# Low-part value matmuls gathered behind a tile's last bank, in an eight-head attention with layer norm in split fp32

## The reference

```python
# x (2048, 256), adj (2048, 2048), Wq, Wk, Wv (256, 2048), Wout (2048, 256), all float32
q = (x @ Wq).reshape(8, 2048, 256)      # likewise k and v
a = einsum('hnd,hmd->hnm', q, k) / 16 + adj + adj
mask = adj == 0
a = softmax(where(mask, -1e6, a)); a = where(mask, 0, a)
out = einsum('hnm,hmd->hnd', a, v).transpose(1, 0, 2).reshape(2048, 2048)
result = layernorm(x + out @ Wout)      # over the last axis, eps 1e-5
```

## Time and profile before

| | |
|---|---|
| median of 3 runs | 1827.27 us (1826.62 to 1828.08) |
| the profiled execution's own time | 1826.6 us, the lowest of the three; its span is the same 1826.6 us |
| busy, share of the span | PE 98%, weight loads 87%, DVE 61%, POOL 54%, ACT 47% |
| PE idle before a value matmul, waiting for POOL's low part | 8.1 us in 7 places |

### The profile page before, as it was taken

One profiled execution on the slowest core, in us unless ns is written; L12 is line 12 of the kernel. 1 busy time (PEld: TensorE's weight loads), 2 busy tenths in 40 slices (PEclk: granted clock), 3 DMA queues, 4 the chain that ended last, 5 costly groups with the idle time before them and its releaser, 6 DMA issues.

```text
span 1826.6 us, 29365 instructions
## 1 busy us (share of the span) xinstructions
PE 1798.8 (98%) x10272; PEld 1582.2 (87%) x10272; DVE 1122.2 (61%) x2318; ACT 852.8 (47%) x1411; POOL 984.9 (54%) x762
## 2 busy tenths in 40 slices
PE   8998989999999999999999999999999999999998
PEld 7887789888898889988899888988889888898887
DVE  6888855665555565555555666555555566546667
ACT  5654554444454445444454444544444444544433
POOL 7878864544644555444554555644455454554443
PEclk9999999999999999999999999999999999999999
DMA  7788875666656666466664666657665566655664
GB/s 250 249 251 267 257 211 154 192 191 195 178 157 185 191 195 186 142 198 194 189 188 142 199 188 190 183 153 201 190 180 173 162 198 196 187 159 169 171 178 140
DMA packets 186995, 345.97 MB, mean 189 GB/s; under 512 B 39392, under 2 KB 96736, under 8 KB 170464
## 3 DMA queue, kind: packets, MB, share of 16 engines
q10 hardware_dynamic: 92032, 200.59, 35.5%
q1 hardware_dynamic: 94816, 143.50, 28.5%
HBM read 190.84 MB, written 18.87 MB: 115 GB/s over the span
## 4 chain that ended last, share of the span: by engine, by line
PE 85%; DVE 1%; SPq 0%; issue 0%; ACT 0%; ACTq 0%; DMA 0%; DVEq 0%
PE bank L400 34%; PE y_bank L417 22%; PE bank L365 17%; PE y_bank L420 12%; SPq L304 0%; DVE y_acc L742 0%; DVE blocks L654 0%; ACTq L567 0%; PE bank L385 0%; DVE p_split L748 0%; DVE y_acc L677 0%; DMA p_turned<-blocks 0%; DVE y_acc L674 0%; ACT m_sb L558 0%; DVE ln L714 0%
## 5 line engine op out<-in xcount | busy, mean ns | idle before, releaser
L471 POOL TENSOR_TENSOR p_split<-p_turned,p_split 128x512 fp32r<-128x512 f32 x510 | 649.7, 1303 | 579.2 <-ACT p_split L539 578.9
L400 PE MATMUL bank<-k_split,q_split 128*128 128x512 f32 x3072 | 794.7, 394 | 0.0
L400 PEld LDWEIGHTS bank<-k_split,q_split 128*128 128x128 f32 x3072 | 546.2, 190 | 90.2
L417 PE MATMUL y_bank<-v_split,p_split 128*128 128x512 f32 x2048 | 549.1, 390 | 8.6 <-POOL p_split L471 8.1
L631 DVE CUSTOM_DVE_ANT_0 t_p<-bank,m_sb 128x512 f32<-128x512 f32 x512 | 350.8, 687 | 231.7 <-PE bank L400 204.5
L417 PEld LDWEIGHTS y_bank<-v_split,p_split 128*128 128x128 f32 x2048 | 382.6, 188 | 92.4 <-POOL p_split L471 11.0
L530 ACT ACTIVATE t_p<-t_p,small 128x2048 f32<-128x2048 f32 x128 | 257.0, 2008 | 392.7 <-DVE small L643 392.7
L460 POOL TENSOR_TENSOR w_slot<-raw_w,w_slot 128x512 fp32r<-128x512 f32 x192 | 250.5, 1305 | 220.7 <-ACT w_slot L510 217.4
L654 DVE STREAM_TRANSPOSE blocks<-t_p 128x2048 f32<-128x2048 f32 x128 | 295.9, 2311 | 97.6 <-ACT t_p L530 77.9
L420 PEld LDWEIGHTS y_bank<-v_split,p_split 128*128 128x128 f32 x2048 | 313.5, 189 | 40.2
L539 ACT ACTIVATE p_split<-p_turned 128x512 fp32r<-128x512 f32 x512 | 287.7, 620 | 86.9 <-DMA p_turned<-blocks 82.8
(11 more groups left out here) (44 smaller groups left out, 644.4 us busy)
## 6 DMA issues: line engine op xcount, KB each, us to landing
m_sb<-m_dram ACTq DMA_DIRECT2D x112, 1024.0 KB, 5.2
p_turned<-blocks SPq DMA_DIRECT2D x1532, 64.0 KB, 2.2
p_turned<-blocks ACTq DMA_DIRECT2D x516, 64.0 KB, 2.8
blocks<-in_adj_dram SPq DMA_DIRECT2D x64, 256.0 KB, 4.2
raw_w<-in_L_gnn_Wv_dram ACTq DMA_DIRECT2D x64, 256.0 KB, 3.4
m_dram<-m_sb SPq DMA_DIRECT2D x16, 1024.0 KB, 6.4
raw_w<-in_L_gnn_Wq_dram ACTq DMA_DIRECT2D x63, 256.0 KB, 3.3
raw_w<-in_L_gnn_Wk_dram ACTq DMA_DIRECT2D x61, 256.0 KB, 4.0
```

The source lines that it names most:

```text
L400: mm = nc.tensor.matmul(dst[:], q[:, a, k, f * P:(f + 1) * P], k_split[:, kk, k, b * BANK:(b + 1) * BANK], start=(i == 0), stop=(i == len( ...
L417: nc.tensor.matmul(y[:], p_split[tau % 2][:, HI, j * P:(j + 1) * P], v_split[:, j].rearrange("p s d -> p (s d)"), start=(j == 0), stop=False)
L471: nc.gpsimd.tensor_tensor(lo, p_turned[:, i * BANK:(i + 1) * BANK].rearrange("p (j b) -> p j b", b=QUAD), hi.bitcast(F32), ALU.subtract).t ...
```

## The change

Three things move; no arithmetic is added or left out, and every matmul keeps its operands.

1. `values` is cut in two. `values_hi` does the wide matmuls in each slot as before and, in slot 0, waits for P's four high parts (`p_hi`) where the four low parts were waited for. `values_lo` does the narrow ones: all 16 of a tile behind the wide ones of slot 3, with the wait for the low parts in front. Only the last tile of a head (but for the very last) keeps four narrow ones in each slot, because v is overwritten there.
2. A head's q projections stand in slot 3 of the even tiles in place of slot 1, and the next head's first q in slot 3 of tile 14 in place of slot 2. They come behind the 16 narrow value matmuls.
3. In later heads the first vt moves from slot 2 of tile 1 to slot 3, in front of the second.

Since `due` orders every engine's work, ACT, DVE and POOL handle the moved projections at the new places too, and the banks of the ring and the weight slots are dealt out in the new order.

```diff
+LO_EVERY = 4
...
-        LATER_V = {(1, 2): (("vt", 0),), (1, 3): (("vt", 1),), (2, 0): (("v", 0), ("vt", 2), ("v", 1), ("vt", 3)),
+        LATER_V = {(1, 3): (("vt", 0), ("vt", 1)), (2, 0): (("v", 0), ("vt", 2), ("v", 1), ("vt", 3)),
...
-            if t % 2 == 0 and t <= LAST_Q and b == (2 if tau == 0 else 1):
+            if t % 2 == 0 and t <= LAST_Q and b == (2 if tau == 0 else 3):
                 yield "q", h, t // 2 + 1
...
-                if (t, b) == (TILES - 2, 2):
+                if (t, b) == (TILES - 2, 3):
                     yield "q", h + 1, 0
...
-                def values(tau, g):
+                def values_hi(tau, g):
                     h, t = divmod(tau, TILES)
                     y = y_bank[tau % 2]
                     if g == 0:
-                        pe.wait_ge(p_lo, 4 * (tau + 1))
+                        pe.wait_ge(p_hi, 4 * (tau + 1))
...
+                def values_lo(tau, first, last):
+                    y = y_bank[tau % 2]
+                    if first == 0:
+                        pe.wait_ge(p_lo, 4 * (tau + 1))
+                    for j in range(TPB * first, TPB * (last + 1)):
                         mm = nc.tensor.matmul(y[:, 0:D], p_split[tau % 2][:, LO, j * P:(j + 1) * P],
                                               v_split[:, j, HI], start=False, stop=(j == CHUNKS - 1))
-                    if g == BANKS - 1:
+                    if last == BANKS - 1:
                         mm.then_inc(y_done, 1)
+
+                def values(tau, g):
+                    values_hi(tau, g)
+                    if tau % TILES == TILES - 1 and tau < ALL - 1:
+                        values_lo(tau, g, g)
+                    elif g % LO_EVERY == LO_EVERY - 1:
+                        values_lo(tau, g + 1 - LO_EVERY, g)
```

More of the change, by code:

```diff
@@ L414, in values @@
                         wait_emptied(("v", h, 2 * g + 1))
-                    chunks = range(TPB * g, TPB * (g + 1))
-                    for j in chunks:
+                    for j in range(TPB * g, TPB * (g + 1)):
                         nc.tensor.matmul(y[:], p_split[tau % 2][:, HI, j * P:(j + 1) * P],
                                          v_split[:, j].rearrange("p s d -> p (s d)"), start=(j == 0), stop=False)
-                    for j in chunks:
+                def values_lo(tau, first, last):
[3 more added lines that the diff above has]
+                    for j in range(TPB * first, TPB * (last + 1)):
                         mm = nc.tensor.matmul(y[:, 0:D], p_split[tau % 2][:, LO, j * P:(j + 1) * P],
                                               v_split[:, j, HI], start=False, stop=(j == CHUNKS - 1))
-                    if g == BANKS - 1:
+                    if last == BANKS - 1:
                         mm.then_inc(y_done, 1)
+                def values(tau, g):
[4 more added lines that the diff above has]
+                        values_lo(tau, g + 1 - LO_EVERY, g)
                 pe.wait_ge(ident_ready, 1)
```

## The result

| | before | after |
|---|---|---|
| median, us | 1827.04 (21 executions, 1824.4 to 1829.27) | 1830.92 (21 executions, 1827.68 to 1836.71) |
| span of the profiled execution, us | 1826.6 | 1827.1 |

The ratio is 1.0022, with a 95% interval of 1.0016 to 1.0028: slower by 3.9 us, where 1.7 was forecast. It is inside the range, at the edge between "within 0.2%" and "slower".

A forecast was written before the change was run, and what follows sets the result against it. PE, busy 98% of the span, was taken as the bound. 1826.6 - 5.4 + 3.6 + 3.0 + 0.5 = 1828.3 us, and 1828.9 for the median; range 1823.5 to 1834.0.

The forecast's parts named there:

- Fewer changes of width: From k2 on, 270 narrow runs among wide matmuls go, each saving about 0.02 us: 5.4 us gained, between 4.5 and 6.
- The rival that nothing is saved: Wide matmuls take as long whatever went before, so grouping gives nothing: 1834.3 us, chance 0.12.
- The wait before k2 at the later ends: Moved q delays ACT's exponential and k2's weight: 0.6 us at six ends of heads 2 to 7, 3.6 us; bounds 0 to 7.2.
- The moved q in the first head: Copies on ACT and DVE delay transposes in tiles 4 and 10 and tile 14's exponential: k2 3.0 us late, bounds 0 to 5.6.
- the forecast's +3.5: First-head loss: 3.0 us by which k2 is late, plus 0.5 us for a longer stretch of low clock.
- the "over 8": Sign of being right: PE idle over 8 us before k2 in the first head.
- The clock: Low-clock stretch at the first head's end may last longer: 0.5 us added, between 0 and 1.7.
- The wait for the high parts: Seven first-head waits end earlier, 3.6 us at one place, but PE then waits for k2's weight: costed at nothing.
- one sign of being wrong: Waits of PE for DVE, a bank or q not emptied, in even tiles.
- What costs nothing: Later heads' other q's (exponential about 1.3 us later, P wanted two tiles on), the moved vt and the tail: no cost.
- the rival "more waits than counted": Weights behind k2's late too (+3.6 us) and first head at its bound (+2.6): up to 1835 us, chance 0.15.

The follow-up runs named there:

- the change with both edits: The full change plus weights split one key earlier and DVE's denominator at slot 2 instead of 0: 1819.95 us, 0.9957 against the kernel before.
- the order alone: Kernel before with only the projections moved (q's, next head's first q, first vt), values as before: 1831.9 us, ratio 1.0027.
- the values alone: Kernel before with values grouped and waiting for high parts, projections unmoved: 1828.19 us, 1.0002; with weights one key earlier 1825.19; with denominator at slot 2 too 1821.07.
- before with the same two edits: Kernel before with weights split one key earlier and DVE's denominator at slot 2 instead of 0: 1822.44 us, ratio 0.9981.
- the whole change: The full change with weights split one key earlier: 1825.99 us, 0.999 against the kernel before; with the denominator at slot 2 too, 1819.95, 0.9957.

## Why the prediction was right and wrong

**Fewer changes of width: right, in mechanism and size.** 0.78 us a head was forecast (39 x 0.02), and the change with both edits shows 222.82 against 223.59. Six scores behind wide value matmuls take 1.36 us, behind narrow ones 1.39. The rival that nothing is saved is refuted. The Trainium skill's page "TensorE: Matmul & The Clock Gate", section "Back-to-back issue gap", gives the formula that the prediction quoted for an isolated matmul, with nothing for what went before; the trace differs from it by the 0.03 us on entry. With the projections at their old places the saving is 0.62 (222.97): seven of the eight q's, and the first vt, stand between wide matmuls there, and each makes a change of width of its own, 8 x 0.02 = 0.16.

**The wait before k2 at the later ends: right.** 0.6 us forecast, 0.56 at every undisturbed end, with the exponential at 1.2 and POOL's weight ahead, as worked out. 223.46 a head is the free 222.82 plus this wait and a little for its weight load.

**The moved q in the first head: right at each place, not in the sum.** From the row maximum to the transpose, the order alone took 4.70, 4.54, 4.85 and 3.48 us in tiles 4, 8, 10 and 14, where before took 3.12, 3.26, 3.42 and 2.52; in tiles 6 and 12, which waited for DMAs, nothing was added. But the 3.0 us on k2 did not show: 233.83 in one execution, in which SP began the shuffles of tile 8 at 152.46, right behind the transpose, where before had held them for 1.5 us; 236.43 in another. k2 was 0.5 us earlier than in before, and 1.8 and 2.1 later. The start of the second head, -1.0, +4.0 and +4.3 us against before in three executions, has the forecast's +3.5 inside its spread, but partly by luck: in the two late ones half of it is the clock's. So this term stands for a mean at best; the profiled execution of after, taken alone, would have called it wrong. PE's idle time before k0 to k2 was 7.6, 7.0 and 5.6 us, less than the "over 8" that was to be the sign.

**The clock: too small in two of three.** 0.5 us was added, 1.7 at most. The low stretch at the first head's end was 3.4 us long in before and in the first profile of after, but 10.2 in the other two, and from k2 to the second head's start they took 16.5 us, where before took 14.3: 2.2 us.

**The wait for the high parts "at nothing": probably too low.** The medians put it at some 3 to 4 us, a gain, with the reserve said above. I argued that none of what paces the first head waits for PE, so that k2's weight alone decides where PE gets to; and I left out that a wait in mid-head can put the next microseconds at half rate. If the gain is real, the total came out near because the next point took it back, which is luck. And one sign of being wrong did show: PE now waits for DVE in four slots of the first head, where before had no such wait, though three of the four are in odd tiles. The same waits stand in the profile of the values alone, which moves no q.

**"What costs nothing": this step failed.** The other q's of the later heads were put at nothing, because P is wanted two tiles on and "PE has shown no wait there", which is no measure of slack. The exponential's 1.4 us became 3.9 at the fourth high copy, and the order alone cost 0.27%. So the rival "more waits than counted" was the missing part, though mostly with other waits than I named. Two kinds have been shown: v7 behind DVE's denominator (0.51 us), and P's high copies that come late from their DMAs, with the weights behind them in ACT's in-order queue (0.6 to 3.1 us of PE's time each, one to three times in an execution of after; one of them had a stretch of low clock after it). In the three profiles of after the longest are where the fourth copy comes latest: 10.5 us into tile 15 (1.9 us of wait), 10.7 (1.3 and 1.9), 11.2 (3.1). With the q's in their old slots none of 36 later heads in six profiles shows a wait of the second kind, and before's heads took 223.59 in all three profiles with its own order.

**The size.** The order alone costs 0.27%, the values alone 0.02%, together 0.22%. Within their intervals the two add up; what didn't come is the values' own gain. In that kernel's profile it is given back by waits for v7 in six later heads. With the slack widened (weights one key earlier, denominator later) the same change gives 1819.95 against 1822.44 us for before with the same two edits, 2.5 us, where 5.4 was the term.

**What stays open.** How the 3.9 us of the median divide between the first head and the later ends: three profiled executions of after, all off its median, don't settle it. Why the denominator's move gave the whole change 6.0 us by the medians (1825.99 to 1819.95), more than the four waits of 0.51 in its profile. And why 2.5 us and not 5.4 are left at the end: from the second head's start on, the profiled execution of the change is 4.8 us shorter than before's, both with the two edits, so the rest must be lost ahead of that or in waits of other executions. The values alone lose as much (4.5 us in that stretch, 1.4 by the medians) and move no q, so the moved q's are not needed to explain it.

## What to carry to other kernels

When the bound engine gets faster or its order shifts, list for each of its waits the slack of today, from the end of the releasing instruction to the start of the waiting one, and test the sum against the jitter of what feeds it; a place where it has never waited may have little left, as v7 had 0.66 us where one collision cost 1.16. Work moved in front of an exponential or a copy in an in-order queue is paid by everything behind it, and a gain on the bound engine is kept only once these links are widened: here two small edits turned +0.22% into -0.43%, of which before gets 0.19 from the same edits. And profile more than one execution when the question is a fifth of a per cent.

## What the runs showed of the hardware

A DVE instruction of one element a partition, with its inputs in SBUF, took up to 1.38 us instead of 0.22 beside POOL's subtractions, and ended with POOL's instruction. So did, within 0.06 us, every one that took over 0.3 us in all fourteen profiles (27 to 91 of the 128 in each). In the values alone its mean over 128 tiles is 0.704 us:

```profile
L673 DVE SCALAR_TENSOR_TENSOR small<-small 128x1 f32<-128x1 f32 x128 | 90.1, 704 | 0.0
```

The page "SBUF — State Buffer" of the Trainium skill, section "Who interferes with whom", says that a DVE instruction with two SBUF inputs and a GpSimd instruction that reads SBUF exclude each other for the whole instruction, whichever came second being blocked. The end times agree with that. The start times don't show who came first: DVE's row starts 0.07 us ahead of POOL's in the slow case (309.68 and 309.75) and 0.06 ahead in the fast one (1204.02 and 1204.08). With the denominator moved no head of any profile waits for v7; for the whole change that is the cure of four such waits, while the values alone had none left in their profile before it.

The granted clock fell to its lower level behind idle times of PE of 1.8 us (the one that ends at 1575.98) and of 3.4 us (ending at 231.72 in the slowest execution, where the next idle time, 2.2 us, fell into the low stretch). Not every such idle time was followed by one: 2.9 us before 1366.78 in the slowest execution, and 3.0 us before k2 in the order alone, were not. In the low stretch a row of six scores shows 2.76 us instead of 1.55; what part of it falls into idle time, where it costs nothing, differed (0.6 of 3.4 us, 2.2 of 10.2). SP's issue of the 12 shuffle DMAs took 7.5 to 9.6 us in the first heads of before and after, so a step of one microsecond there may be swallowed in one execution and passed on in the next.
